# Second attention's transfer order, and its opening beside the feed-forward stage's last stores

## What is computed

```
x = layernorm(x + attention0(x))     # 16 heads of 16, q and k normalised, rotary positions
x = layernorm(x + ffn0(x))           # silu(x Wg) * (x Wu), then Wd
x = layernorm(x + attention1(x))     # 8 heads of 32, causal, an extra rank-one term in the scores
x = layernorm(x + experts(x))        # 16 experts, the best 2 of each token, capacity 512
```

## Time and profile before

| | us |
|---|---|
| median of 3 runs (1964.29 to 1966.22) | 1966.1 |
| the profiled execution | 1972.85 |
| its span, from the first to the last instruction | 1971.1 |
| PE busy | 1813.4 (92%) |
| DVE busy | 1428.9 (72%) |
| ACT busy | 1124.2 (57%) |
| GpSimd busy | 510.7 (26%) |
| granted TensorE clock, mean | 0.945 of full |

### The profile page before, as it was taken

How to read it: one execution, slowest core, us unless ns; L and a number is a source line. 1 busy time by engine, 2 the same in 40 slices (tenths; PEclk the granted TensorE clock), 3 DMA queues, 4 the chain that set the end, 5 groups by cost and what they waited for, 6 DMA issues and landing times. The chain is left out here.

```text
span 1971.1 us, 34758 instructions
## 1 busy us (share of the span) xinstructions
PE 1813.4 (92%) x12676; PEld 1181.2 (60%) x12676; DVE 1428.9 (72%) x2803; ACT 1124.2 (57%) x2228; POOL 510.7 (26%) x648
## 2 busy tenths in 40 slices
PE   8979999999999999799999869898999868899992
PEld 4545444444444444688888745564555457899992
DVE  7869999999999996467766555565656454566663
ACT  4635888888888889323222215454544523655554
POOL 5750000332000001223221122114324243344441
PEclk9976999999999999899999969989989989999996
DMA  4883734654353302115434454646545253555645
GB/s 168 289 239 46 116 82 93 143 137 127 62 82 72 63 19 82 41 52 176 136 107 132 154 141 110 140 94 165 125 127 135 69 164 109 136 141 145 157 91 184
DMA packets 169717, 238.99 MB, mean 121 GB/s; under 512 B 25689, under 2 KB 109178, under 8 KB 169568
## 3 DMA queue, kind: packets, MB, share of 16 engines
q1 hardware_dynamic: 138256, 178.82, 37.1%
q0 software_dynamic: 15200, 26.76, 5.8%
q10 hardware_dynamic: 16112, 31.46, 4.5%
HBM read 136.97 MB, written 96.60 MB: 118 GB/s over the span
## 5 line engine op out<-in xcount | busy, mean ns | idle before, releaser
L988 DVE TENSOR_REDUCE b_mx<-b_PM 128x1 f32<-128x512 f32 x1024 | 621.1, 683 | 22.3 <-PE b_PM L842 21.9
L964 ACT ACTIVATE b_probs<-b_PS 128x512 f32<-128x512 f32 x1000 | 523.9, 606 | 69.0 <-PE b_PS L896 53.5
L2781 ACT ACTIVATE d_probs<-d_PS 128x512 f32<-128x512 f32 (+3 forms) x384 | 166.7, 496 | 202.7 <-PE d_PS L2693 202.1
L842 PE MATMUL b_PM<-b_kst,b_qst 48*128 48x512 f32 x888 | 281.4, 431 | 0.0
L2821 DVE TENSOR_REDUCE d_mx<-d_PM 128x2 f32<-128x1024 f32 (+1 forms) x192 | 180.1, 951 | 114.9 <-PE d_PM L2645 68.7
L896 PE MATMUL b_PS<-b_qst,b_kst 50*128 50x512 f32 x744 | 257.0, 437 | 1.8
L896 PEld LDWEIGHTS b_PS<-b_qst,b_kst 50*128 50x128 f32 x744 | 120.5, 184 | 163.4 <-ACT b_probs L964 147.8
L2744 POOL TENSOR_SCALAR_AFFINE_SELECT d_probs<-d_probs 128x128 f32<-128x128 f32 x256 | 77.7, 317 | 271.5 <-ACT d_probs L2781 267.1
L868 PE MATMUL b_PO<-b_probs,x_v 128*32 128x384 f32 (+2 forms) x2048 | 145.2, 390 | 0.0
L842 PEld LDWEIGHTS b_PM<-b_kst,b_qst 48*128 48x128 f32 x888 | 142.1, 185 | 5.3
L868 PE MATMUL b_PO<-b_probs,b_vst 128*32 128x384 f32 (+3 forms) x1960 | 143.0, 397 | 1.0 <-ACT b_probs L964 0.9
(11 more groups left out here) (300 smaller groups left out, 3761.8 us busy)
## 6 DMA issues: line engine op xcount, KB each, us to landing
halves<-a_parts SPq DMA_DIRECT2D x7, 2048.0 KB, 8.7
qk<-c_halves ACTq DMA_DIRECT2D x7, 2048.0 KB, 12.4
w_w<-L_ffn_fc1T SPq DMA_DIRECT2D x12, 1024.0 KB, 4.9
w_w<-L_ffn_fc2T SPq DMA_DIRECT2D x12, 1024.0 KB, 6.4
b_qst<-halves SPq DMA_DIRECT2D x72, 128.0 KB, 4.4
b_kst<-halves SPq DMA_DIRECT2D x72, 128.0 KB, 7.6
d_qst<-qk SPq DMA_DIRECT2D x36, 256.0 KB, 4.7
d_kst<-qk SPq DMA_DIRECT2D x36, 256.0 KB, 6.9
```

The lines of the kernel that those rows point to most:

```text
L842: mm = pe.matmul(PM[n % MBANKS][:], qst[buf][at, p, first:first + P], kst[buf][at, p, kh * BLK:(kh + 1) * BLK], start=True, stop=True)
L964: act.activation(probs[:, s % RING], score_bank(g, s)[:], ACT.Exp).then_inc(exped, 1)
L988: dve.tensor_reduce(mx[:, half, (r * PAIRS0 + p) * TPH + t, kh:kh + 1], PM[n % MBANKS][:], AX.X, ALU.max)\
L2781: act.activation(probs[:, s % RING, 0:w], PS[bank(s)][:, 0:w], ACT.Exp).then_inc(exped, 1)
```

## The change

SP no longer waits for the last six stores of the feed-forward stage: they count on a semaphore that both stages share, and in the next stage SP waits for it before its first load, and GpSimd before it sets the ones rows. In SP's order the load of group g+3 stands before the share load and store. The token stores move from the third to the fourth group of a sequence. The router's exponential moves from tick 29 to tick 30; DVE's sum, inverse and multiplication behind it stand together in tick 31.

```diff
+    FFN_DMAS = 16 * (1 + 1 + 4)
@@ phase_ffn0, sync: the x2 store
+                      .then_inc(x2_out[i] if n < BLOCKS - 1 else shared.ffn_stored, 16)
@@ the four pieces of qk1
-                  .then_inc(last_out, 16)
+                  .then_inc(shared.ffn_stored, 16)
-            for i in range(2):
-                for s in (x2_out, v_out):
-                    sp.wait_ge(s[i], 16 * BATCH + 16)
+            for s in (x2_out, v_out):
+                sp.wait_ge(s[0], 16 * BATCH + 16)
+                sp.wait_ge(s[1], 16 * BATCH)
             sp.wait_ge(halves_out, 16 * BLOCKS)
-            sp.wait_ge(last_out, 16 * 4)
@@ scalar: the v1 store
+                       .then_inc(v_out[i] if n < BLOCKS - 1 else shared.ffn_stored, 16)
@@ Routing
-    LOGITS, EXPS, RANKS = 27, 29, 39
+    LOGITS, EXPS, RANKS = 27, 30, 39
-    LAST_ACT = {24: (20,), 25: (22,), 26: (23,), 30: (24,), EXPS + BEHIND: (29,)}
+    LAST_ACT = {24: (20,), 25: (22,), 26: (23,), 30: (24,), EXPS + BEHIND: (30,)}
-        if k == self.LOGITS + 3:
+        if k == self.EXPS + 1:
             dve.wait_ge(self.expd_done, u + 1)
...
-        if k == self.LOGITS + 4:
             past(5)
@@ phase_layer1, sync
+            sp.wait_ge(shared.ffn_stored, shared.FFN_DMAS)
             load(1)
...
                 if g + 1 < GROUPS:
                     rows(g + 1)
+                if g + BUFS - 1 < GROUPS:
+                    if g > 0:
+                        sp.wait_ge(pv_done, g * ROUNDS + RING // G1)
+                    load(g + BUFS - 1)
                 if g > 0:
                     route.load_shares(sp, d, g - 1, 1)
                 route.store_shares(sp, d, g, 0)
-                if g + BUFS - 1 < GROUPS:
-                    if g > 0:
-                        sp.wait_ge(pv_done, g * ROUNDS + RING // G1)
-                    load(g + BUFS - 1)
+                b = g // HG1
                 if g % HG1 == HG1 - 2:
-                    b = g // HG1
                     route.load_tokens(sp, d, b)
-                    if b > 0:
-                        for n in range((b - 1) * HPS, b * HPS):
-                            tokens.store(sp, d, n)
+                if g % HG1 == HG1 - 1 and b > 0:
+                    for n in range((b - 1) * HPS, b * HPS):
+                        tokens.store(sp, d, n)
@@ gpsimd
+            pool.wait_ge(setup, 2)
+            pool.wait_ge(shared.ffn_stored, shared.FFN_DMAS)
             for i in range(BUFS):
                 pool.memset(kst[i][K:KM].bitcast(F32), 1.0).then_inc(ones_set, 1)
-            pool.wait_ge(setup, 2)
```

More of the change, by code:

```diff
@@ L474, in __init__ @@
         self.att2T = nc.alloc_sbuf_tensor_at("x_att2T", [P, HALVES1, CD, BLK], F32R, offset=top - 17 * 1024)
-        self.bproj_in, self.last_stored = a.sem("bproj_in"), a.sem("last_stored")
+        self.bproj_in, self.last_stored, self.ffn_stored = a.sem("bproj_in"), a.sem("last_stored"), a.sem("ffn_stored")
         self.weighed, self.biased = a.sem("weighed"), a.sem("biased")
@@ L1172, in phase_ffn0 @@
         x2_out = [a.sem(f"x2_out{i}") for i in range(2)]
-        halves_out, last_out = a.sem("halves_out"), a.sem("last_out")
+        halves_out = a.sem("halves_out")
         v_out = [a.sem(f"v_out{i}") for i in range(2)]
@@ L1212, in step @@
                     sp.wait_ge(S["x2_done"], (n + 1) * TPK)
-                    sp.dma_start(d["x2"][tok, :].rearrange("(t p) c -> p t c", p=P), x2[:, i]).then_inc(x2_out[i], 16)
+                    sp.dma_start(d["x2"][tok, :].rearrange("(t p) c -> p t c", p=P), x2[:, i])\
+                      .then_inc(x2_out[i] if n < BLOCKS - 1 else shared.ffn_stored, 16)
             block_pipeline(sp, step, LAG)
@@ L1415, in step @@
                     act.dma_start(d["v1"][tok, :].rearrange("(t p) c -> p t c", p=P),
-                                  vaug[:, i].rearrange("p t h c -> p t (h c)")).then_inc(v_out[i], 16)
+                                  vaug[:, i].rearrange("p t h c -> p t (h c)"))\
+                       .then_inc(v_out[i] if n < BLOCKS - 1 else shared.ffn_stored, 16)
                     if n < BLOCKS - 1:
@@ L2597, in _ @@
                     rows(g + 1)
-                if g > 0:
-                    route.load_shares(sp, d, g - 1, 1)
-                route.store_shares(sp, d, g, 0)
                 if g + BUFS - 1 < GROUPS:
@@ L2605, in _ @@
                     load(g + BUFS - 1)
+                if g > 0:
+                    route.load_shares(sp, d, g - 1, 1)
+                route.store_shares(sp, d, g, 0)
+                b = g // HG1
                 if g % HG1 == HG1 - 2:
-                    b = g // HG1
                     route.load_tokens(sp, d, b)
-                    if b > 0:
-                        for n in range((b - 1) * HPS, b * HPS):
-                            tokens.store(sp, d, n)
+                if g % HG1 == HG1 - 1 and b > 0:
+                    for n in range((b - 1) * HPS, b * HPS):
+                        tokens.store(sp, d, n)
             route.load_shares(sp, d, GROUPS - 1, 0)
```

## The result

| | before | changed |
|---|---|---|
| median of the comparison, 15 runs each | 1966.2 us (1962.9 to 1972.6) | 1972.2 us (1969.7 to 1980.1) |
| ratio to before, 95% interval | | 1.0035 (1.0024 to 1.0046) |
| profiled execution, its span | 1972.9, 1971.1 | 1971.9, 1970.2 |
| first product of the second attention | 1144.1 | 1137.6 |
| group periods 0→4 together | 88.0 | 81.3 |

The forecast was 1955 with a range to 1966; the change costs 6 us (0.35%). The last four lines of the table are read from the timelines; a period n→m runs from ACT's copy of round 6 in group n to that in group m, as under the earlier trace rows. They tell most of the story: the groups that were to get faster did, and the price stands in three places, each time just behind the end of a sequence.

What follows compares the result with a forecast made beforehand. PE was taken to bound the second attention (364 of 395 us busy, clock 0.93). Terms -5.5 - 8.0 - 7.0 - 7 - 2 + 15 + 3 + 0.5 = -11 gave 1955 us against the 1966.1 median, range 1940 to 1966.

Steps and rivals of the forecast that it cites:

- shares behind the load: Groups 5, 9 and 13, tick 12: share loads queue behind the 2 MB load and land late, +15 us (3 to 28).
- Opening, -5.5: Start of the second attention: SP's wait for the last store's landing goes from the barrier, 5.5 us less.
- full clock in the opening: Rival, chance 0.07: PE's shorter stand before the second attention keeps its clock up, some 4 us more gained, 1951.
- Loads before shares -8.0: Second attention: the load of group g+3 starts earlier, so all of PE's waits for keys go, 8.0 us less.
- totals -7.0: Groups 7 and 11: PE's two 3.5 us waits, from totals queued behind load, `x2` and token stores, go.
- clock -7: Second attention: half-clock stretches behind PE's waits in groups 7 and 11, 4 and 12 go, 7 us less.
- Exponential, -2: Router, a tick later: ACT's wait for DVE's subtraction in group 14, and PE's behind it, go, 2 us less.
- clock +3: Half-clock stretches behind PE's new waits for late shares, in two of three places, +3 us (0 to 5).
- The tail, +0.5: End of the second attention: token stores in group 15 stand before the share load, +0.5 us (0 to 4).
- shares hold the routing: Rival, chance 0.10: in groups 5, 9 and 13 shares come 9.3 us late, lateness handed on by each group, 1973.6.
- Only the opening and the exponential: Rival, chance 0.12: DMA engines stay the limit, keys and totals come as late as before, 1961.
- Shares come in time: Rival, chance 0.17: the shares' lateness is 1.1 us only and the totals' slide nil, 1940.

## Why the prediction was wrong

Nearly each mechanism was where it was forecast. What failed is the size of the cost: the term "shares behind the load" with its clock, +18, which measured 27, and in it what the moved token stores do, which was priced at next to nothing there and at +0.5 at the end.

*Opening, -5.5:* right, measured -7.5 alone. The rival of a full clock in the opening is out: the clock is 0.50 from 1137.6 to 1153.6 as it was.

*Loads before shares -8.0, totals -7.0, clock -7:* as gains they came. Set against the trace of before, the periods 0→4, 7→8 and 11→12 gave 6.7 + 7.4 + 8.6 = 22.7 us, forecast 22. But the order alone gives all but 1 us of that, so the stores' departure, which was to bring part of the -7.0, was not what brought it. And the waits that the totals cause did not go: they left groups 7 and 11, and with the moved stores PE has one of 2.96 and one of 4.16 us in 8 and 12.

*Exponential, -2:* fits, with -2.4 measured and an interval that nearly reaches 0.

*Shares behind the load, +15, with clock +3:* **the term that failed.** The periods 4→5, 8→9 and 12→13 grew by 5.3 + 11.1 + 10.5 = 26.9 us against the 18 of the sum. The windows of the three periods split that into PE's idle time and its busy time for the same products, which grows only with the half clock. Here is 8→9, before, with the order alone and in the changed kernel:

```profile
1379.80:1408.65 28.85, 27.28 (x147) 17.60 (x145) 18.39 (x32) 11.39 (x29) 11.30 (x22) 1.00 0.56 142
...
1369.72:1408.50 38.78, 32.32 (x146) 20.15 (x145) 18.75 (x33) 11.41 (x29) 11.75 (x23) 0.87 0.41 106
...
1364.42:1404.42 40.00, 30.71 (x146) 19.32 (x145) 18.56 (x33) 11.49 (x29) 10.88 (x22) 0.87 0.46 120
```

| PE busy + idle, us | before | order alone | changed |
|---|---|---|---|
| 4→5 | 30.3 + 1.3 | 29.0 + 6.1 | 30.6 + 6.3 |
| 8→9 | 27.3 + 1.6 | 32.3 + 6.5 | 30.7 + 9.3 |
| 12→13 | 30.3 + 1.3 | 32.3 + 6.5 | 32.1 + 10.0 |
| sum, growth over before | | busy +5.7, idle +14.8 | busy +5.5, idle +21.4 |

Two things come out. With the order alone the three places are alike, and the idle time grows by 14.8 us, the +15 of the sum; but the clock costs 5.7 and not 3. And the changed kernel adds 6.3 us of growth, all of it idle time, which lies nearly whole in 8→9 and 12→13, the two periods that follow groups with moved stores. There SP issues the stores for 7.6 and 9.0 us before it sends the totals, DVE waits 6.31 and 7.51 us for them, and PE 2.96 and 4.16 for DVE. The prediction had named the stores as something that slides the totals, and gave the slide 1.5 us "as most groups have no `x2` or token DMAs"; two of the three places that it priced have the stores in the group before.

The ratios say the same. The order, the opening and the exponential, each alone, add up to nothing (+0.49, -0.38 and -0.12%), and the changed kernel has +0.35%. So the moved stores, which alone cost 0.03%, cost some 7 us beside the other parts, with an uncertainty of 5. No run takes them out of the changed kernel with its narrow share loads, so this rests on the sum of the ratios and on the periods.

*Against which execution.* The sum of -11 was taken from before's profiled 1972.9, and then its 6.8 us above the median as well. The excess is not spread evenly. The trace of the exponential alone lies at its own median: there 0→4 takes 86.2 us (not 88.0), 11→12 27.7 (not 28.9) and 5→6 29.4 (not 31.8). Against it the change gave 4.9 + 7.4 + 7.4 = 19.7 us, 3 less than against the other. The prediction took away an execution's bad luck, and then once more as a gain. The two profiled executions alone differ by only 0.9 us (1972.9 and 1971.9) because the first was an unlucky one.

*The tail, +0.5:* from the second attention's last copy to the experts' first product it took 66.6 us, and 64.6 before, and the rest of the span 1.9 more, 3.9 in all. The token stores alone show the same, 3.5 us more than the exponential alone on the same chip. With wide share loads the stores stand in the same place, and the tail is 390.2 and 390.6 us, as it was before with 389.8. But the kernel with narrow share loads first has them there too, and its tail of 397.8 is that of the order alone on the same chip, 397.9. So the moved stores may be the cause, near the upper bound of 4 that this term was given, but it stays open; each figure is one execution's.

Together: 9 us from the shares, the clock and the stores, 3 from the execution, 3 or so from the tail, less 2 for the opening, are 13 of the 17 by which the forecast missed; the rest lies in periods such as 6→7 and 13→14 that differ by 1 to 2 us and that no run isolates.

*The rivals.* The slower one (shares hold the routing: 1973.6) had the place, tick 12 of groups 5, 9 and 13, and the sign and nearly the time, and its clock (+5) and its end (+4) were measured at 5.5 and 3.9. But its chain was not what happened. It had every group handing on its lateness, so that the shares come 9.3 us late; here DVE waited for 3.5, 4.7 and 4.2 us for them, and what came on top were the totals behind the stores, in two places. That its time was nearly met is in part luck. "Only the opening and the exponential" is ruled out by the periods, which did change, and "the barrier waits for the landings" by the opening alone. "Shares come in time" is ruled out by the 17.8 us.

The narrow load was in the prediction, as a rule beside a lateness of 2 us per place. The runs show it was worth more: widening gave 21 us in the changed kernel and 19 with the shares ahead. The rule was weighed for the load's own landing alone, and not for what stands behind it. That is measured for the values' load, which lands 2.1 us earlier in the median, and for SP's issue of the stores, 3.5 to 4.2 us shorter each time. From the first product of the stage to its last copy the kernel with wide shares first takes 409.6 us and the one with narrow shares first 426.4; of these 16.9 us PE's busy time, and so the clock, makes 9.6, and idle time 7.3. How much of that each transfer brings was not measured.

## What to carry to other kernels

Before changing the order of transfers, look at how wide each one is: here 128 KB with an outermost dimension of 2 made the 2 MB behind them late, and neither place in the order was right for them until they were widened. When a change moves two things, price them together too: the stores cost nothing alone and some 7 us beside the new order. When a step recurs at several places, price each place with what else stands there in the queue. And where the profiled execution is above the median, part of its excess may sit in just the waits that a change would free, as 3 of 6.8 us did here, so take the gains from an execution near the median.

## What the runs showed of the hardware

A share load of 128 KB over two rows took 3 us of transfer at 46 GB/s with next to nothing beside it; as two calls over 32 partitions each, 64 KB landed 2.4 us after their issue in the median. Widening these loads was worth 3.7 us in the old order, 21 behind the keys' load and 19 ahead of it. The issue itself can hold SP: two token stores of 512 KB took it 7.6 and 9.0 us behind the 2 MB load and narrow shares, 10.5 and 10.7 with narrow shares ahead of that load, 6.7 and 7.2 with wide ones ahead, and in that order 1.2 and 1.4 a group earlier.

The granted clock follows PE's waits: with none for the weighing or the maxima above 1.6 us its mean in the stage's middle rose from 0.93 to 0.97. From the first product to the last copy PE was busy 386.9 us for the same products, where the changed kernel took 398.5, and idle 22.7 instead of 40.4: of the 29.4 us gained there 11.7 came with the clock and 17.7 with the waits.

And a stretch that the edits hardly touch, from the second attention's last copy to the experts' first product, took 64.1 to 66.9 us in the six traces of before, of the changed kernel and of the second batch, and 71.5 to 72.7 in the eight of the first and third, whatever the kernel. By that grouping it is taken for a difference between chips, by which spans of different batches can't be set against each other.
